# Query norms applied to the scores, the window mask added by TensorE, and a shifted TensorE loop in an AdaLN block

## The chip, the cores and the metric

The kernel runs on one core of a Trainium2 chip. The metric is the device time of one execution in microseconds, lower is better. A core has five engines that take their instructions from queues of their own: TensorE (PE), VectorE (DVE), ScalarE (ACT), GpSimd (POOL) and SyncE (SP), which here starts the DMAs. They meet only at semaphores: an instruction may wait until a counter has a value, and may raise one when it is done.

## The reference

The block has two halves. The first is a layer norm with modulation and a causal attention of 16 heads over an input of 8 batches x 512 tokens x 128 columns. The second, which this change touches, is a stack of six layers of local attention and a gated feed-forward:

```python
q = l2norm(q) * qs                      # per token and head, 64 columns
k = l2norm(k) * ksc
q = q * cos * scale + rotate_half(q) * sin * scale
k = k * cos * inv + rotate_half(k) * sin * inv
sim = jnp.einsum('bhwie,bhwje->bhwij', bq, bk2) * QK_SCALE
sim = jnp.where(mask, -jnp.finfo(sim.dtype).max, sim)   # window of 32, one window back
attn = jax.nn.softmax(sim, -1)
out = jnp.einsum('bhwij,bhwje->bhwie', attn, bv2)
...
for i in range(DEPTH):                  # DEPTH = 6
    x = attn_layer(shift_tokens(x), ...) + x
    x = ffn_layer(shift_tokens(x), ...) + x
```

`l2norm` divides a head's 64 numbers by their norm. One number per token and head does it, so for the query it may be applied to the scores of that token and head as well as to the query itself.

## The kernel before

Three parts run one after the other: `modulated_attention` (names `at_...`), `local_stack` (names `st_...`) and `last_residual` (`lr_...`). Only the second is changed. It works on units: a unit is one batch in one layer, 6 x 8 = 48 of them. Units 0 and 1 and the last ones are written out; units 2 to 46 are 45 passes of a hardware loop (L292). A unit has four tiles of 128 tokens, t = 0 to 3, so there are 192 tiles.

The order of the work is written by hand in `jobs_of` (L247). In each step t TensorE does, in this order: `q` of tile t, `tq` (transposing the rotated query of tile t-1), `k`, `tk`, `v`, `ot` (transposing the attention output of tile t-3), `pt` (transposing the probabilities of t-2), `sim` (the scores of t-1, 32 small matmuls per tile, L457), one job of the feed-forward (`m2` at t = 0, none at t = 1, `y` at t = 2, `m1` at t = 3), `z` (the output projection of t-3), `o` (probabilities times values of t-2), and at t = 1 the three blocks `h` of the feed-forward's first matmul. Each job owns PSUM banks: `q` 0 and 1, `k` and `o` 4 and 5, `tq`, `v` and `sim` 2 and 3, `tk` and `pt` 6 and 7, `ot` 0 and 1, `m1`, `m2` and `y` 7, `z` 6. `slot_free` makes a job wait until what stood in its banks has been read.

Around it, in step t:
- ScalarE squares q (L537), copies the transposed query (L559), squares k, copies the transposed keys into a block-diagonal tensor (L568), takes the exponential of the scores of t-2 (L573), copies v (L582), `ot` (L592) and `pt` (L598), and computes the reciprocal norms' first guess (L545, L547).
- VectorE sums the squares (L668), multiplies q and k by the cosines (L672) and sines (L686), clamps the sums (L679), adds the mask to the scores of t-1 while it takes them out of PSUM (L707), takes their maximum (L711), and divides the attention output by the softmax's sum (L749 to L759). At t = 1 it begins with a product of the feed-forward's norm (L656) and later finishes that norm (L736); the products of `hid` are L769.
- GpSimd adds the two parts of the rotation (L789, for q and k), refines the reciprocal norms (L796 to L802), multiplies the rotated q and then k by them (L809, `normalise`), and subtracts the maximum from the scores of t-1 (L837). At t = 1 it first does four operations for the feed-forward's norm (L816 to L824).

TensorE's `tq` waits for `normed[0]`, raised by the product for q in L809; `tk` for `normed[1]`.

Of the kernel before, what the change touches and what calls it, by code (L numbers as in the profile page):

```python
# [7 lines left out]
ALU = mybir.AluOpType  # L8
# [33 lines left out]

MASKED = -3.0e38


# [8 lines left out]


def shape_constants():

# [7 lines left out]
    first = seen & ((np.arange(P)[:, None] >= WIN) | (j >= WIN))  # L65
    c[:, C_MASK:C_MASK + 2 * WIN] = np.where(first, 0.0, MASKED)
    c[:, C_MASK + 2 * WIN:C_MASK + 4 * WIN] = np.where(seen, 0.0, MASKED)
    c[:, C_CAUSAL:C_CAUSAL + P] = np.where(np.arange(P)[None, :] <= np.arange(P)[:, None], 0.0, MASKED)
# [43 lines left out]
def local_stack(nc, w, LAYERS, const_sb, xT, x_done, w_split, tables):  # L112
# [68 lines left out]
    with ExitStack() as ctx:  # L181
# [36 lines left out]
        hid = sb("hid", [P, HC, N])  # L218

        ps = ctx.enter_context(nc.psum_tensor("st_ps", [P, NBANKS * BANK], F32))  # L220


        small_in, wo_in, w12_in = sem("small_in"), sem("wo_in"), sem("w12_in")
        wqkv_in = {k: sem(f"w{k}_in") for k in "qkv"}
# [16 lines left out]
        ff_squared, ff_rstd, ff_xn = sem("ff_squared"), sem("ff_rstd"), sem("ff_xn")  # L241
        gelu_ready = sem("gelu_ready")
        ff_gain, ff_newton, pool_own = sem("ff_gain"), sem("ff_newton"), sem("pool_own")
# [43 lines left out]

        def loop(eng, unit):

            unit(0)  # L290
            unit(1)
            with eng.Fori(2, NU - 1) as u:  # L292
                unit(u)
            unit(NU - 1)
            unit(NU)
            unit(NU + 1)

        with nc.Block() as block:
# [101 lines left out]
            def _(pe):  # L400
                pe.wait_ge(zeroed, 2)

                pe.sem_inc(ready["o"], 2)

                def unit(u):
                    for t in range(TILES):
                        at = STARTS[t]

                        for i, ((kind, d, index), _) in enumerate(jobs_of(t)):
# [29 lines left out]
                            elif kind in ("tq", "tk"):  # L439

                                pe.wait_ge(normed[kind == "tk"], tiles_done(u, d, index))
                                src = qk_rot[:, (kind == "tk") * INNER:(1 + (kind == "tk")) * INNER]
# [7 lines left out]
                            elif kind == "sim":  # L450
# [3 lines left out]
                                for c in range(IC):  # L454
                                    for g in range(WPT):
                                        key = index * P + g * WIN
                                        last = pe.matmul(  # L457
                                            out[g * WIN:(g + 1) * WIN, c * P:(c + 1) * P],
                                            qT[:, par, c * P + g * WIN:c * P + (g + 1) * WIN],
                                            k_bd[:, c, :, key:key + 2 * WIN], start=True, stop=True)  # L460
                            elif kind == "o":
# [43 lines left out]

                loop(pe, unit)

            @block.scalar
            def _(act):

                act.preload_act_table_set(EXP_LN_SET)
                act.wait_ge(small_in, 64)
                act.wait_ge(zeroed, 3)

                def round_half(u, d, half):
# [12 lines left out]
                def unit(u):  # L528
                    for t in range(TILES):
# [9 lines left out]
                        def reciprocal_norm():  # L539

                            act.wait_ge(ss_ready, n)
                            if not (start and n < 3):
                                act.wait_ge(normed[1], n - 2)
                            r = rn[:, t % 2, :]
                            act.activation(r, ss[:, t % 2, :], ACT.Ln, scale=SS_SCALE).then_inc(rn_ready, 1)  # L545
# [80 lines left out]

                loop(act, unit)

            @block.vector
            def _(dve):  # L630
# [17 lines left out]
                def unit(u):  # L648
                    start = isinstance(u, int)
                    for t in range(TILES):  # L650
# [7 lines left out]
                        def rotate(a):  # L658
# [7 lines left out]
                            if not (start and n < 3):  # L666
                                dve.wait_ge(normed[a], n - 2)
                            dve.tensor_reduce(nt[:, 2 + par, heads], qk_sq[:, cols].rearrange("p (h d) -> p h d", d=DH),  # L668
# [30 lines left out]
                        if alive(u, d1):  # L699
# [72 lines left out]

                loop(dve, unit)

            @block.gpsimd
            def _(pool):
                pool.wait_ge(small_in, 64)

                def unit(u):
                    start = isinstance(u, int)  # L780
                    for t in range(TILES):
# [57 lines left out]

                loop(pool, unit)  # L840

# [19 lines left out]
def modulated_attention(nc, w, const_sb, mod, xT, x_done, x1_dram, w_split, tables):  # L861
# [28 lines left out]
    with ExitStack() as ctx:  # L890
# [40 lines left out]
        ps_m = bank("m")  # L931

        w_in, x_in, x1_out, scale_in = sem("w_in"), sem("x_in"), sem("x1_out"), sem("scale_in")
        tables_done, tables_out = sem("tables_done"), sem("tables_out")
# [32 lines left out]

        def loop(eng, batch):

            batch(-1)  # L970
            batch(0)
            with eng.Fori(1, BATCH - 1) as b:
                batch(b)
            batch(BATCH - 1)
            batch(BATCH)

        with nc.Block() as block:
# [59 lines left out]
            def _(pe):  # L1037
# [103 lines left out]

                loop(pe, batch)

            @block.scalar
            def _(act):
# [71 lines left out]

                loop(act, batch)

            @block.vector  # L1220
            def _(dve):
# [162 lines left out]

                loop(dve, batch)

            @block.gpsimd
            def _(pool):
# [40 lines left out]

                loop(pool, batch)  # L1430

# [113 lines left out]
```

## Time and profile before

| what | value |
| --- | --- |
| runs of the kernel | 4410.03, 4414.46, 4418.47 us, median 4414.46 |
| the profiled execution | 4412.12 us, its span 4410.3 us |
| TensorE clock granted, mean | 0.959 of full speed |
| PE busy | 3768.9 us (85%) |
| PE's weight loads busy | 2856.2 us (65%) |
| DVE busy | 3571.7 us (81%) |
| ACT busy | 2656.4 us (60%) |
| POOL busy | 2895.4 us (66%) |
| `sim` matmuls, L457 | 376.1 us |
| q, k, v matmuls, L429 | 956.7 us |
| POOL's products with the norms, L809 | 722.7 us, x384 |

The span runs from the first to the last instruction of the profiled execution. The stack begins at about 880 us; its loop runs from about 1019 to 4250 us. A busy share is an average over the whole program; what a change is worth must be read where the engines wait for each other.

### The profile page before, as it was taken

What the parts mean: (1) busy time and instruction counts of PE and PEld (TensorE: products, weight loads), DVE (VectorE), ACT (ScalarE), POOL (GpSimd) and SP (SyncE); (2) the same over time, 40 slices, a digit from 0 to 9 for tenths busy, and PEclk for the clock granted to TensorE, in tenths of its full rate; (3) what the DMA queues carried; (4) which work ended last, traced back from release to release, by engine and by line L of the source; (5) the groups of instructions that cost most, each with busy time, mean ns of one, the idle gap of its engine ahead of it and who ended that gap; (6) DMA issues with size and microseconds to landing.
All of it is one profiled execution on the core that took longest, in us unless ns stands there. A gap on an engine that the chain in (4) does not pass through costs nothing. (4 is left out here: it accounts for less than half of the span.)

```text
span 4410.3 us, 109941 instructions
## 1 busy us (share of the span) xinstructions
PE 3768.9 (85%) x41516; PEld 2856.2 (65%) x41516; DVE 3571.7 (81%) x5298; ACT 2656.4 (60%) x4035; POOL 2895.4 (66%) x2520
## 2 busy tenths in 40 slices
PE   5666666669999899998999989999899999899996
PEld 3444444357777777776777767777677777677774
DVE  6777777678888788887888878888888888888884
ACT  5666666546666566656566656656566656566663
POOL 3555555357777677676767666777677676667672
PEclk9888888889999999999999999999999999999998
DMA  1111111032222322223222232222322222222221
GB/s 38 53 53 53 53 53 45 8 90 64 55 60 56 92 59 62 56 58 91 62 55 62 56 88 65 55 58 54 89 60 67 56 56 78 70 60 63 56 55 58
DMA packets 157205, 267.21 MB, mean 61 GB/s; under 512 B 32062, under 2 KB 51644, under 8 KB 152380
## 3 DMA queue, kind: packets, MB, share of 16 engines
q1 hardware_dynamic: 157116, 266.19, 22.1%
q8 instruction: 36, 0.59, 0.1%
q14 instruction: 53, 0.43, 0.0%
HBM read 44.81 MB, written 26.21 MB: 16 GB/s over the span
## 5 line engine op out<-in xcount | busy, mean ns | idle before, releaser
L789 POOL TENSOR_TENSOR st_qk_rot<-st_qk_rot,st_qk_sq 128x1024 f32<-128x1024 f32 x384 | 920.4, 2397 | 939.6 <-DVE st_qk_sq L686 939.6
L429 PE MATMUL st_ps<-st_wqkv,st_xs 128*128 128x512 f32 x3456 | 956.7, 412 | 66.2 <-DMA st_wqkv<-wqkv_parts 37.7
L537 ACT ACTIVATE st_qk_sq<-st_ps 128x1024 f32<-128x1024 f32 x384 | 393.9, 1026 | 652.6 <-PE st_ps L429 652.0
L429 PEld LDWEIGHTS st_ps<-st_wqkv,st_xs 128*128 128x128 f32 x3456 | 612.4, 190 | 231.4 <-issue 97.8
L809 POOL TENSOR_TENSOR st_qk_rot<-st_qk_rot,st_rn 128x1024 f32<-128x1024 f32 x384 | 722.7, 1903 | 15.0
L1426 POOL TENSOR_TENSOR at_probs<-at_probs,at_rden 128x128 f32<-128x128 f32 (+3 forms) x512 | 361.8, 738 | 389.6 <-DVE at_rden L1357 389.6
L668 DVE TENSOR_REDUCE st_nt<-st_qk_sq 128x16 f32<-128x1024 f32 x384 | 465.7, 1213 | 175.5 <-ACT st_qk_sq L537 175.4
L686 DVE TENSOR_TENSOR st_qk_sq<-st_ps,st_rot 128x512 f32<-128x512 f32 x768 | 490.2, 678 | 0.0
L672 DVE TENSOR_TENSOR st_qk_rot<-st_ps,st_rot 128x1024 f32<-128x1024 f32 x384 | 465.9, 1213 | 8.6 <-PE st_ps L444 8.6
L444 PE MATMUL st_ps<-consts_sb,st_qk_rot 128*128 128x128 f32 x3072 | 403.0, 274 | 27.9 <-DVE st_hid L769 16.5
L437 PEld LDWEIGHTS st_ps<-st_oT,st_wo 128*128 128x128 f32 x3072 | 368.8, 192 | 79.4 <-issue 75.8
L1191 ACT ACTIVATE at_probs<-at_score,at_nmx 128x128 f32<-128x128 f32 (+3 forms) x512 | 269.1, 527 | 249.0 <-DVE at_nmx L1347 244.3
L444 PEld LDWEIGHTS st_ps<-consts_sb,st_qk_rot 128*128 128x128 f32 x3072 | 357.1, 141 | 93.7 <-DVE st_hid L769 36.3
L568 ACT ACTIVATE st_k_bd<-st_ps 64x1024 f32<-64x1024 f32 x384 | 389.4, 1014 | 3.7 <-PE st_ps L444 1.4
L437 PE MATMUL st_ps<-st_oT,st_wo 128*128 128x128 f32 x3072 | 379.2, 277 | 1.4 <-ACT st_probT L598 1.2
L457 PE MATMUL st_ps<-st_k_bd,st_qT 128*32 128x128 f32 x12288 | 376.1, 275 | 1.8 <-ACT st_v_tok L582 1.8
L1056 PE MATMUL at_score<-at_k,at_qm 128*128 128x128 f32 (+3 forms) x512 | 239.9, 510 | 159.8 <-ACT at_probs L1191 117.6
L469 PE MATMUL st_ps<-st_v_bd,st_probT 128*32 128x128 f32 x12288 | 375.2, 274 | 0.0
L837 POOL TENSOR_TENSOR st_s<-st_s,st_mx 128x1024 f32<-128x1024 f32 x192 | 365.8, 1905 | 9.9 <-DVE st_mx L711 9.9
L707 DVE TENSOR_TENSOR st_s<-st_ps,consts_sb 128x1024 f32<-128x1024 f32 x192 | 234.5, 1221 | 146.4 <-PE st_ps L457 146.4
L457 PEld LDWEIGHTS st_ps<-st_k_bd,st_qT 128*32 128x32 f32 x12288 | 324.4, 110 | 34.4 <-ACT st_v_tok L582 26.2
L469 PEld LDWEIGHTS st_ps<-st_v_bd,st_probT 128*32 128x32 f32 x12288 | 323.8, 110 | 23.0
(125 smaller groups left out, 6828.4 us busy)
## 6 DMA issues: line engine op xcount, KB each, us to landing
st_v_bd<-st_v_tok SPq DMA_DIRECT2D x1152, 128.0 KB, 2.3
st_v_bd<-st_v_tok SPq DMA_DIRECT2D x672, 64.0 KB, 2.1
wqkv_parts<-at_w_parts SPq DMA_DIRECT2D x18, 1024.0 KB, 4.5
st_wqkv<-wqkv_parts SPq DMA_DIRECT2D x18, 1024.0 KB, 5.7
at_w_raw<-in_wqkv SPq DMA_DIRECT2D x18, 512.0 KB, 4.1
rotary_tables<-at_rot SPq DMA_DIRECT2D x6, 512.0 KB, 2.8
st_rot<-rotary_tables SPq DMA_DIRECT2D x24, 128.0 KB, 2.4
st_wo<-in_wo SPq DMA_DIRECT2D x6, 512.0 KB, 4.2
```

Source lines behind the costliest of these rows:

```text
L429: last = pe.matmul(out[:, c * 512:(c + 1) * 512], xs[:, x_part, t * P:(t + 1) * P], rhs, start=(n == 0), stop=(n == len(PASSES) - 1))
L437: last = pe.matmul(out[:, 0:P], wo[:, c, :], oT[:, c * P:(c + 1) * P], start=(c == 0), stop=(c == IC - 1))
L444: last = pe.transpose(out[:, c * P:(c + 1) * P], src[:, c * P:(c + 1) * P], ident)
L457: last = pe.matmul(out[g * WIN:(g + 1) * WIN, c * P:(c + 1) * P], qT[:, par, c * P + g * WIN:c * P + (g + 1) * WIN], k_bd[:, c, :, key:key ...
L469: last = pe.matmul(out[g * WIN:(g + 1) * WIN, c * P:(c + 1) * P], probT[:, c * P + g * WIN:c * P + (g + 1) * WIN], v_bd[:, par, g, :, c * ...
L537: act.activation(qk_sq[:, cols_of(a)], slot_of("qk"[a], 0, t), ACT.Square).then_inc(squared[a], 1)
L568: last = act.activation(k_bd[rows, :, a, WIN + t1 * P:WIN + (t1 + 1) * P], src[rows, :, :], ACT.Copy)
L668: dve.tensor_reduce(nt[:, 2 + par, heads], qk_sq[:, cols].rearrange("p (h d) -> p h d", d=DH), AX.X, ALU.add).then_inc(ss_sum, 1)
L672: dve.tensor_tensor(qk_rot[:, cols].rearrange("p (h d) -> p h d", d=DH), slot_of("qk"[a], 0, t).rearrange("p (h d) -> p h d", d=DH), rot[: ...
L686: last = dve.tensor_tensor(dst[:, :, g, :], src[:, :, 1 - g, :], sines.unsqueeze(1).to_broadcast([P, HEADS, DH // 2]), ALU.mult)
L789: pool.tensor_tensor(qk_rot[:, cols], qk_rot[:, cols], qk_sq[:, cols], ALU.add).then_inc(rot_done[a], 1)
L809: pool.tensor_tensor(view, view, rn[:, par, heads_of(a)].unsqueeze(2).to_broadcast([P, HEADS, DH]), ALU.mult).then_inc(normed[a], 1)
```

## The change

Four things are changed in `local_stack`:

1. GpSimd no longer multiplies q by its reciprocal norms; `tq` waits for the rotation of q alone (`rot_done[0]`).
2. VectorE's instruction that takes the scores out of PSUM multiplies them by those norms, broadcast over 64 columns, instead of adding the mask. Three waits go with it, since the norms are now read later.
3. The mask is added by TensorE: behind the 32 small matmuls of `sim`, which now leave their accumulation open, two matmuls multiply the identity (128 x 128) with the mask, broadcast over eight heads (512 columns), into the same banks. The mask's value becomes -1e30. ScalarE writes the identity and the two masks once as float32r, and TensorE waits for this.
4. 139 instructions that raise a semaphore nobody waits for stand on TensorE's queue before unit 0 (`ST_FILL`).

```diff
+AT_FILL = {}
+ST_FILL = {"pe": 139}
+def fill_block(eng, filled, n):
+    for _ in range(n):
+        eng.sem_inc(filled, 1)
...
+        ident_r, mask_r = sb("ident_r", [P, P], F32R), sb("mask_r", [P, 2, 2 * WIN], F32R)
...
-        def loop(eng, unit):
-
+        def loop(eng, unit, fill=0):
+
+            fill_block(eng, filled, fill)
             unit(0)
...
                 pe.wait_ge(zeroed, 2)
+                pe.wait_ge(rounded, 3)
...
-                                pe.wait_ge(normed[kind == "tk"], tiles_done(u, d, index))
+                                pe.wait_ge(normed[1] if kind == "tk" else rot_done[0], tiles_done(u, d, index))
...
-                                            k_bd[:, c, :, key:key + 2 * WIN], start=True, stop=True)
+                                            k_bd[:, c, :, key:key + 2 * WIN], start=(c % 4 == 0), stop=False)
+                                for c in range(2):
+                                    last = pe.matmul(out[:, c * 512:(c + 1) * 512].rearrange("p (h k) -> p h k", k=2 * WIN),
+                                                     ident_r[:, :],
+                                                     mask_r[:, index > 0, :].unsqueeze(1).to_broadcast([P, HEADS // 2, 2 * WIN]),
+                                                     start=False, stop=True)
...
+                act.activation(ident_r[:, :], ident, ACT.Copy).then_inc(rounded, 1)
+                for i in range(2):
+                    act.activation(mask_r[:, i, :], mask[i], ACT.Copy).then_inc(rounded, 1)
...
                                 act.wait_ge(normed[1], n - 2)
+                                act.wait_ge(taken["sim"], n - 2)
...
-                                dve.wait_ge(normed[a], n - 2)
+                                dve.wait_ge(rn_final, n - 2)
...
+                            dve.wait_ge(rn_final, n - 1)
                             dve.tensor_tensor(scores, slot_of("sim", d1, t1).rearrange("p (h k) -> p h k", h=HEADS),
-                                              mask[0 if t1 == 0 else 1].unsqueeze(1).to_broadcast([P, HEADS, 2 * WIN]),
-                                              ALU.add).then_inc(taken["sim"], 1)
+                                              rn[:, par, heads_of(0)].unsqueeze(2).to_broadcast([P, HEADS, 2 * WIN]),
+                                              ALU.mult).then_inc(taken["sim"], 1)
...
                             reciprocal_norms()
-                            normalise(0)
                             normalise(1)
```

How TensorE's queue moves, in the loop's pass at t = 2 (`st_s` are the scores, `st_o` the attention output, `st_hid` the feed-forward's hidden values). Before:

```order
L477 MATMUL st_ps<-consts_sb,st_o 128x128 x8
L449 MATMUL st_ps<-consts_sb,st_s 128x128 x8
L457 MATMUL st_ps<-st_k_bd,st_qT 32x128 x32
L502 MATMUL st_ps<-st_hid,st_w 128x512 x3
L437 MATMUL st_ps<-st_oT,st_wo 128x128 x8
```

and in the changed kernel, whose line numbers are higher:

```order
L499 MATMUL st_ps<-consts_sb,st_o 128x128 x8
L466 MATMUL st_ps<-consts_sb,st_s 128x128 x8
L474 MATMUL st_ps<-st_k_bd,st_qT 32x128 x32
L479 MATMUL st_ps<-st_mask_r,st_ident_r 128x512 x2
L524 MATMUL st_ps<-st_hid,st_w 128x512 x3
L454 MATMUL st_ps<-st_oT,st_wo 128x128 x8
```

The two matmuls with the mask stand between the scores and the next job, in all four steps; nothing else has moved there.

GpSimd's queue in one step, before (`st_qk_rot` is the rotated q and k, `st_rn` the norms, `st_mx` the maxima):

```order
L789 TENSOR_TENSOR st_qk_rot<-st_qk_rot,st_qk_sq 128x1024 x2
L793 REGISTER_ALU
L796 TENSOR_TENSOR st_nt<-st_rn 128x32
L797 ISA
L798 TENSOR_TENSOR st_nt<-st_nt,st_ss 128x32
L799 REGISTER_ALU
L800 TENSOR_TENSOR st_nt<-consts_sb,st_nt 128x32
L802 TENSOR_TENSOR st_rn<-st_rn,st_nt 128x32
L809 TENSOR_TENSOR st_qk_rot<-st_qk_rot,st_rn 128x1024 x2
L837 TENSOR_TENSOR st_s<-st_s,st_mx 128x1024
```

and in the changed kernel:

```order
L816 TENSOR_TENSOR st_qk_rot<-st_qk_rot,st_qk_sq 128x1024 x2
L820 REGISTER_ALU
L823 TENSOR_TENSOR st_nt<-st_rn 128x32
L824 ISA
L825 TENSOR_TENSOR st_nt<-st_nt,st_ss 128x32
L826 REGISTER_ALU
L827 TENSOR_TENSOR st_nt<-consts_sb,st_nt 128x32
L829 TENSOR_TENSOR st_rn<-st_rn,st_nt 128x32
L836 TENSOR_TENSOR st_qk_rot<-st_qk_rot,st_rn 128x1024
L863 TENSOR_TENSOR st_s<-st_s,st_mx 128x1024
```

One product of 128 x 1024 less stands ahead of the subtraction of the maxima.

## Rows read from the trace of the kernel before

**Rows 1.** Busy time by stretch: the stack's loop, 1110 to 4250 us.
```profile
1110.00:4250.00 3140.00, 2884.59 (x34868) 2260.20 (x34871) 2657.69 (x3280) 1929.19 (x2361) 2215.11 (x1750) 0.99 0.25 64
```
**Rows 2.** Waits, whole run: engine, line, waited for, total us, times, longest.
```profile
PE st_ps L477 <- issue: 112.3, 183, 1.6
...
PE st_ps L449 <- ACT st_s L573: 86.8, 145, 2.4
...
PEld st_ps L502 <- ACT st_probT L598: 18.6, 46, 0.4
...
PEld st_ps L486 <- ACT st_probT L598: 16.8, 41, 0.4
```
**Rows 3.** Timeline of TensorE, one pass: start us, us, instruction, idle before.
```profile
3076.22 1.96 PE L457 MATMUL st_ps<-st_k_bd,st_qT 128*32 128x128 f32 x64
3078.32 2.84 PE L502 MATMUL st_ps<-st_hid,st_w 128*128 128x512 f32 x6
...
3087.05 1.63 PE L429 MATMUL st_ps<-st_wqkv,st_xs 128*128 128x512 f32 x6
3088.52 1.03 PE L444 MATMUL st_ps<-consts_sb,st_qk_rot 128*128 128x128 f32 x8
...
3093.90 1.95 PE L457 MATMUL st_ps<-st_k_bd,st_qT 128*32 128x128 f32 x64
3095.84 1.12 PE L481 MATMUL st_ps<-xT_sb,consts_sb 128*128 x2
3096.80 1.95 PE L437 MATMUL st_ps<-st_oT,st_wo 128*128 128x128 f32 x16
...
3124.33 1.07 PE L477 MATMUL st_ps<-consts_sb,st_o 128*128 128x128 f32 x8 [1.61 <-issue]
3125.24 1.04 PE L449 MATMUL st_ps<-consts_sb,st_s 128*128 128x128 f32 x8
3126.20 1.95 PE L457 MATMUL st_ps<-st_k_bd,st_qT 128*32 128x128 f32 x64
3128.09 2.05 PE L437 MATMUL st_ps<-st_oT,st_wo 128*128 128x128 f32 x16
...
3132.26 1.12 PE L494 MATMUL st_ps<-st_xc,st_w 128*128 128x512 f32 x2 [0.24 <-DVE st_xc L736]
```
**Rows 4.** Timeline of VectorE in the same pass, from the end of t = 0.
```profile
3117.18 1.23 DVE L759 TENSOR_TENSOR st_o<-st_ps,st_den 128x1024 f32<-128x1024 f32 x1
3118.32 2.46 DVE L656 SCALAR_TENSOR_TENSOR st_xc<-st_xc,st_ln_g,st_rstd 128x512 f32<-128x512 f32 x1
...
3122.96 1.27 DVE L686 TENSOR_TENSOR st_qk_sq<-st_ps,st_rot 128x512 f32<-128x512 f32 x2
...
3129.09 1.21 DVE L707 TENSOR_TENSOR st_s<-st_ps,consts_sb 128x1024 f32<-128x1024 f32 x1
```
**Rows 5.** Timeline of GpSimd over the same time.
```profile
3114.60 3.77 POOL L809 TENSOR_TENSOR st_qk_rot<-st_qk_rot,st_rn 128x1024 f32<-128x1024 f32 x2
3118.32 1.91 POOL L837 TENSOR_TENSOR st_s<-st_s,st_mx 128x1024 f32<-128x1024 f32 x1
3120.19 1.49 POOL L816 TENSOR_TENSOR st_xc<-st_rstd 128x512 f32<-128x512 f32 x1
```
**Rows 6.** Timeline of ScalarE at t = 1 of the same pass.
```profile
3123.47 1.06 ACT L573 ACTIVATE st_s<-st_s 128x1024 f32<-128x1024 f32 x1
```
**Rows 7.** One line's instructions, L656: duration ns min/median/max, first and last start.
```profile
L656 DVE SCALAR_TENSOR_TENSOR st_xc<-st_xc,st_ln_g,st_rstd x48: 741/2473/2498, 1037.6 to 4363.6; 128x512 f32<-128x512 f32 x48
```
**Rows 8.** Who waited for GpSimd's products L809, whole run: us, times.
```profile
  PE st_ps L444: 11.3, 3
```
**Rows 9.** One line's instructions, L403: TensorE's queue raises a semaphore.
```profile
L403 PEldq EVENT_SEMAPHORE  x1: 51/51/51, 895.8 to 895.8; - x1
```
**Rows 10.** DMA queues over the whole run: packets, MB, share.
```profile
q8 instruction: 36, 0.59, 0.1%
```
**Rows 11.** The same for 1110 to 4260 us: the only instruction queue listed.
```profile
q14 instruction: 3, 0.02, 0.0%
```

More of the change, by code:

```diff
@@ L43 @@
 MASKED = -3.0e38
+MASKED_SCORE = -1.0e30
 C_IDENT, C_MEAN, C_MASK, C_CAUSAL = 0, P, 2 * P, 2 * P + 4 * WIN
@@ L65, in shape_constants @@
     first = seen & ((np.arange(P)[:, None] >= WIN) | (j >= WIN))
-    c[:, C_MASK:C_MASK + 2 * WIN] = np.where(first, 0.0, MASKED)
-    c[:, C_MASK + 2 * WIN:C_MASK + 4 * WIN] = np.where(seen, 0.0, MASKED)
+    c[:, C_MASK:C_MASK + 2 * WIN] = np.where(first, 0.0, MASKED_SCORE)
+    c[:, C_MASK + 2 * WIN:C_MASK + 4 * WIN] = np.where(seen, 0.0, MASKED_SCORE)
     c[:, C_CAUSAL:C_CAUSAL + P] = np.where(np.arange(P)[None, :] <= np.arange(P)[:, None], 0.0, MASKED)
@@ L218, in local_stack @@
         hid = sb("hid", [P, HC, N])
+        ident_r, mask_r = sb("ident_r", [P, P], F32R), sb("mask_r", [P, 2, 2 * WIN], F32R)
         ps = ctx.enter_context(nc.psum_tensor("st_ps", [P, NBANKS * BANK], F32))
+        filled = sem("filled")
         small_in, wo_in, w12_in = sem("small_in"), sem("wo_in"), sem("w12_in")
@@ L241, in local_stack @@
         ff_squared, ff_rstd, ff_xn = sem("ff_squared"), sem("ff_rstd"), sem("ff_xn")
-        gelu_ready = sem("gelu_ready")
+        gelu_ready, rounded = sem("gelu_ready"), sem("rounded")
         ff_gain, ff_newton, pool_own = sem("ff_gain"), sem("ff_newton"), sem("pool_own")
@@ L504, in unit @@
                             last.then_inc(ready[kind], 1)
-                loop(pe, unit)
+                loop(pe, unit, ST_FILL.get('pe', 0))
             @block.scalar
@@ L625, in unit @@
                             act.preload_act_table_set(EXP_LN_SET)
-                loop(act, unit)
+                loop(act, unit, ST_FILL.get('act', 0))
             @block.vector
@@ L771, in unit @@
                                                          ALU.add, ALU.mult).then_inc(taken["h"], 1)
-                loop(dve, unit)
+                loop(dve, unit, ST_FILL.get('dve', 0))
             @block.gpsimd
@@ L838, in unit @@
                                                ALU.subtract).then_inc(shifted, 1)
-                loop(pool, unit)
+                loop(pool, unit, ST_FILL.get('pool', 0))
 AH = 16
@@ L931, in modulated_attention @@
         ps_m = bank("m")
+        filled = sem("filled")
         w_in, x_in, x1_out, scale_in = sem("w_in"), sem("x_in"), sem("x1_out"), sem("scale_in")
@@ L966, in jobs_at, with loop @@
                     if (step, p) == (s % AH, part) and (not kinds or kind in kinds)]
-        def loop(eng, batch):
+        def loop(eng, batch, fill=0):
+            fill_block(eng, filled, fill)
             batch(-1)
@@ L1140, in batch @@
                         m_products(b, s, 1)
-                loop(pe, batch)
+                loop(pe, batch, AT_FILL.get('pe', 0))
             @block.scalar
@@ L1216, in batch @@
                                     take(b, job)
-                loop(act, batch)
+                loop(act, batch, AT_FILL.get('act', 0))
             @block.vector
@@ L1383, in batch @@
                             finish_norm(b, -1, True)
-                loop(dve, batch)
+                loop(dve, batch, AT_FILL.get('dve', 0))
             @block.gpsimd
@@ L1428, in batch @@
                         last.then_inc(weights_ready, 1)
-                loop(pool, batch)
+                loop(pool, batch, AT_FILL.get('pool', 0))
 def last_residual(nc, const_sb, mod, xT, x1_dram, out):
```

## The prediction

> **What bounds the kernel now.** First I read the busy time by stretch. In the 3140 us from 1110 to 4250 TensorE is busy 2885 us, 92%, at a granted clock of 0.99 (its level of 2.4 GHz); VectorE has 85%, GpSimd 71%, ScalarE 61% [rows 1]. So the loop is close to TensorE's own time, and the question is what ends TensorE's few gaps. The view of waits names two: before `ot` (L477) it stands 112.3 us in 183 cases, before `pt` (L449) 86.8 us in 145 cases, for the exponential [rows 2]. "issue" on the first hides a wait: `ot` takes the banks of q, so it needs VectorE's sine product of q (L686), and the timeline shows that one end at 3122.96 + 1.27 = 3124.23 and `ot` start at 3124.33 [rows 3, 4]. Neither chain (q matmul, square, sum, two products; k matmul, square, key copy, exponential) has GpSimd in it. GpSimd's products with the norms, of which the change removes half, made anyone wait for 11.3 us in 3 cases in the whole run [rows 8]. What GpSimd gives up is thus off the path, but for one place that the timeline shows at t = 1, below.
>
> **The mask pair on TensorE.** Two float32r matmuls of 512 columns per tile. The nearest row is the projection: six of that shape and type from 3087.05 to the next start at 3088.52, 1.47/6 = 0.245 us each [rows 3]; the pair costs m = 0.49 us. Below it could only go if they overlapped the scores; above, a float32 matmul of 512 columns took 3096.80 - 3095.84 = 0.96 us [rows 3], so a pair of 1.92 us if the broadcast mask streamed at that pace. I take 0.49, with 0.45 to 0.60 as its own range: same engine, type and width. 192 tiles would make 94 us, but each of the four steps of a pass must be walked, S being how much later TensorE is than before, from `h` of one pass to `h` of the next.
>
> - t = 2: behind the scores comes `y`, which waits for ScalarE's copy L598 [rows 2]: from the scores' start to its start 2.10 us (3076.22, 3078.32), against 1.88 where nothing is waited for (3126.20, 3128.09) [rows 3]. The pair fills that 0.22: +0.27.
> - t = 3: scores to `m1` 1.94 us (3093.90, 3095.84), 0.06 hidden: +0.43. S = 0.70.
> - t = 0: `m2` waits for the same copy as `y` (16.8 us in 41 cases, beside 18.6 in 46 [rows 2]): +0.27. S = 0.97.
> - t = 1: `ot` stood 1.61 us [rows 3], since VectorE was late: L759 ended and L656 took 2.46 us instead of the 0.74 that is its minimum [rows 4, 7]. It ended 0.6 us after GpSimd's L837 did (3118.32 + 1.91 = 3120.23; 3120.78) [rows 4, 5]: it had to let that instruction, which reads SBUF too, go first.
>
>  With the change VectorE reaches L656 at 3118.32 + S(t = 3) 0.70 + m 0.49 = 3119.51. GpSimd, also 0.70 later but one product (3.77/2 = 1.88 us) shorter [rows 5], ends L837 at 3120.23 + 0.70 - 1.88 = 3119.05 and goes on with L816, 1.04 to 1.49 us. L656 then waits for that instead: it ends at about 3119.1 + 1.2 + 0.6 = 3120.9, as late as before. So `ot` keeps its time and the 0.97 is swallowed. Late next is the exponential: it ended at 3123.47 + 1.06 = 3124.53 [rows 6], is S later, 3125.50, and 0.1 us behind it (as `ot` behind L686) `pt` can start, 3125.60 against 3125.24: +0.36. The pair follows: +0.85 at `z`. `h` waited about 0.31 us for VectorE's L736 (from `z` to `h` 3132.26 - 3128.09 = 4.17 us, where `z` and `o` fill 1.98 + 1.88) [rows 3]; that wait goes: +0.54, with the roundings 0.56.
>
> In a formula the next `h` is 4m - 1.4 us later, 0.56 with m = 0.49. 46 passes of full content make 25.8 us. Two units of the ramps without a feed-forward pay nearly the full 4m: +3.5.
>
> The Trainium skill (SBUF — State Buffer, section "SBUF: two separate sides") states that VectorE and GpSimd share one pair of ports as an exclusive lock, held for the whole instruction, so that a VectorE operation with two SBUF inputs fully blocks behind a GpSimd one. The trace agrees for L656: 2.46 us against 0.74. By that rule L679, a small clamp, also shortens at t = 1, which is not late for anyone and changes no term.
>
> **VectorE's product instead of the sum.** Same shape, PSUM in, one SBUF operand broadcast. The product with the softmax's reciprocal (L759), of just that form, took 1.23 us, the sum 1.21 us [rows 4]: nothing, +-0.02 x 192 = 4 us at most, and VectorE waits for the scores in three steps of four. At t = 1, where L707 stood right behind L686 (3129.09), it now finds the scores ready at about 3129.0: no loss. The wait for the norms is behind GpSimd's work of the step before; behind it queue the maximum and `z`'s addition, but it is met long before the scores are. ScalarE's new wait for `taken["sim"]` asks for a tile two back. Both cost nothing.
>
> **Start of the stack.** 139 semaphore instructions; the nearest row is 51 ns for one that TensorE's queue executed [rows 9]: 7.1 us, at most; at least 0, if they pass while TensorE waits for its first input. They stand behind the wait for ScalarE's rounding, so little is left to hide them: I take +6.5. Against it stand the 11.3 us [rows 8] that `tq` and `tk` waited for the products in the first tiles: the change takes 1.9 us off each `tk` and more off `tq`; I take -6. Bounds for both together: -11 to +8. Sum: 25.8 + 3.5 + 0.5 = +30 us.
>
> **Where the loop stands.** Queue q8 moved 36 packets in the whole run, 16 KB each, and none from 1110 to 4260 us [rows 10, 11]. I read it as TensorE's program: its loop is held on the chip, and moving it to a border can gain nothing against before. It can only keep that state, since a pass grows by 16 instructions. The Trainium skill (Runtime: NRT & Kernel Launch, "Instruction fetch mechanics") says that a taken branch whose target is outside a window of two blocks of 256 instructions forces a fetch; TensorE's pass, some 1,670 instructions, would then be fetched anew 45 times. The empty q8 in rows 11 speaks against it for TensorE.
>
> The profiled execution took 4412.12 us (span 4410.3 and 1.8 around it); the median of the runs is 2.3 us above it, less than their spread. 4412.1 + 30 = 4442 us.
>
> **Rivals.**
> - A, the forecast: m from 0.45 to 0.60 gives 0.40 to 1.00 us a pass, 18 to 46 us, with the rest (+4) 4434 to 4462.
> - B, faster: the pair costs TensorE less than it replaces in gaps. It decides from 4m = 1.4, m = 0.35. For it: 64 narrow score matmuls leave room between them, and wide ones might slip in. Against: they come behind the scores in one queue, and 512 columns took 0.245 us each with no gap between them. At m = 0.20: -0.60 x 46 = -28, with the rest 4388.
> - N, no change: m near 0.35, or the start gives back all of the 11.3 us; 4404 to 4421.
> - D, t = 1 swallows nothing: L656 starts 1.19 us later and still takes 2.46 us, because GpSimd goes on with its next instruction before it gives way. Then `ot` is 1.19 later, and a pass 1.19 + 0.49 - 0.31 = 1.37 us: 63 us, with the rest 4479. For it: GpSimd's operations stand nearly without gaps. Against: L656 did get in between L837 and L816.
> - C, the change doesn't do what it says: the loop now touches one block too many, and TensorE fetches in each pass. The trace of before shows no such stall; 36 packets took 0.1% of 16 engines' span [rows 10], 0.05 to 0.15% before rounding, so 1 to 3 us each; one waited for per pass is 45 us or more on top of A: 4487 and up.
> - E, the mask streams at the float32 pace: 4 x 1.92 - 1.4 = 6.3 us a pass, 4706.
>
> **Chances.** A 0.50, D 0.15, C 0.07, E 0.03, N 0.11, B 0.14. A measurement of this kernel tells 0.2%, 9 us, from nothing. A, D, C and E are slower by more: 0.75; N 0.11; B 0.14. The range takes in A, D and N and part of B and C: 4398 to 4492, with A's own 4434 to 4462.
>
> **What would show it.** The new matmuls at 0.24 to 0.25 us from start to start; the pair's 0.49 between the scores and `y`, `m1`, `m2`, `z`; `y` and `m2` no longer waiting for L598; L656 at 1.2 to 1.6 us; `ot` at t = 1 with a gap of 0.6 us in place of 1.6, and a new gap of 0.2 us for the exponential before `pt`; L736 no longer named before `h`; a pass 0.6 us longer; no q8 packet in the loop. I am wrong if a pass is shorter than before, which would need a gap before `ot` or `pt` in t = 2, 3 or 0 to have shrunk, or if TensorE's queue stalls at the loop's branch.

## The result and the profile after

The changed kernel takes 4520.64 us (median of 4 runs, 4516.04 to 4530.03), the kernel before in the same session 4413.16 us: ratio 1.0245, 95% interval [1.0225, 1.0265]. It is 107 us slower. The prediction was 4442 us, range 4398 to 4492: the sign was right, the size 3.6 times too small.

The same stretch of the loop as in [rows 1], then the page's engine line. Columns of the first: TensorE, its weight loads, VectorE, ScalarE and GpSimd busy, the granted clock, the DMA share, GB/s.

```profile
1110.00:4250.00 3140.00, 2887.94 (x34403) 2267.68 (x34402) 2559.82 (x3193) 1874.07 (x2300) 1840.87 (x1539) 0.99 0.24 63
```
```profile
PE 3867.7 (86%) x41900; PEld 2930.7 (65%) x41900; DVE 3537.3 (78%) x5298; ACT 2652.3 (59%) x4038; POOL 2532.3 (56%) x2328
```

TensorE is as full as before, at the same clock, with 1.3% fewer instructions in the stretch; GpSimd has given up 374 us of work there, and yet a pass is longer, as the next rows show.

One pass of TensorE, from `h` to `h`. This is the counterpart of [rows 3]; columns: start, duration, instruction, and in brackets the gap before it and what ended it.

```profile
3070.02 5.41 PE L516 MATMUL st_ps<-st_xc,st_w 128*128 128x512 f32 x12 [1.17 <-DVE st_xc L763]
...
3102.83 1.95 PE L474 MATMUL st_ps<-st_k_bd,st_qT 128*32 128x128 f32 x64
3104.72 0.73 PE L479 MATMUL st_ps<-st_mask_r,st_ident_r 128*128 128x512 f32 x2
3105.29 1.02 PE L503 MATMUL st_ps<-xT_sb,consts_sb 128*128 x2
3106.15 1.95 PE L454 MATMUL st_ps<-st_oT,st_wo 128*128 128x128 f32 x16
...
3132.85 1.06 PE L499 MATMUL st_ps<-consts_sb,st_o 128*128 128x128 f32 x8 [0.51 <-issue]
3134.31 1.07 PE L466 MATMUL st_ps<-consts_sb,st_s 128*128 128x128 f32 x8 [0.39 <-ACT st_s L599]
3135.30 1.95 PE L474 MATMUL st_ps<-st_k_bd,st_qT 128*32 128x128 f32 x64
3137.19 0.73 PE L479 MATMUL st_ps<-st_mask_r,st_ident_r 128*128 128x512 f32 x2
3137.76 1.95 PE L454 MATMUL st_ps<-st_oT,st_wo 128*128 128x128 f32 x16
3139.63 1.96 PE L491 MATMUL st_ps<-st_v_bd,st_probT 128*32 128x128 f32 x64
3142.77 5.41 PE L516 MATMUL st_ps<-st_xc,st_w 128*128 128x512 f32 x12 [1.18 <-DVE st_xc L763]
```

A pass takes 3142.77 - 3070.02 = 72.75 us. Before, the `h` at 3132.26 [rows 3] followed this one, 70.93 us earlier:

```profile
3061.33 5.41 PE L494 MATMUL st_ps<-st_xc,st_w 128*128 128x512 f32 x12 [0.24 <-issue]
```

All but every eighth pass of either kernel repeat these lengths, with medians of 72.74 and 70.95 us; the eighth, where the layer changes, is 7 to 8 us longer before and 8 to 9 us longer after. So a pass pays 1.79 us, 45 x 1.79 = 81 us, where I had forecast 0.56. The five layer changes pay about 1 us each on top of it.

The gap before `ot` at t = 1 has shrunk to 0.51 us and a gap of 0.39 us stands before `pt`, as forecast. What is new is the last row: `h` waits 1.18 us for VectorE's L763 (L736 in the kernel before). The waits of the whole run, to be read beside [rows 2]; columns: who waits, for whom, us in total, times, longest:

```profile
PE st_ps L466 <- ACT st_s L599: 100.5, 186, 2.1
...
PE st_ps L499 <- issue: 68.0, 181, 0.6
...
PE st_ps L516 <- DVE st_xc L763: 53.4, 45, 1.2
...
PE st_ps L446 <- issue: 46.8, 1, 46.8
```

45 passes, 53.4 us. Why L763 is late stands in VectorE's and GpSimd's timelines of this pass. VectorE:

```profile
3128.23 1.06 DVE L682 SCALAR_TENSOR_TENSOR st_xc<-st_xc,st_ln_g,st_rstd 128x512 f32<-128x512 f32 x1
...
3134.93 0.45 DVE L705 TENSOR_SCALAR st_ss<-st_nt 128x32 f32<-128x32 f32 x1
3135.30 1.27 DVE L712 TENSOR_TENSOR st_qk_sq<-st_ps,st_rot 128x512 f32<-128x512 f32 x2
3137.95 1.22 DVE L734 TENSOR_TENSOR st_s<-st_ps,st_rn 128x1024 f32<-128x1024 f32 x1 [1.38 <-PE st_ps L479]
3139.21 1.22 DVE L738 TENSOR_REDUCE st_mx<-st_s 128x16 f32<-128x1024 f32 x1
3140.35 2.11 DVE L763 TENSOR_SCALAR st_xc<-st_xc,st_ln_b 128x512 f32<-128x512 f32 x1
```

GpSimd:

```profile
3127.70 1.04 POOL L843 TENSOR_TENSOR st_xc<-st_rstd 128x512 f32<-128x512 f32 x1
...
3136.65 2.37 POOL L816 TENSOR_TENSOR st_qk_rot<-st_qk_rot,st_qk_sq 128x1024 f32<-128x1024 f32 x1 [1.31 <-DVE st_qk_sq L712]
...
3140.28 1.90 POOL L836 TENSOR_TENSOR st_qk_rot<-st_qk_rot,st_rn 128x1024 f32<-128x1024 f32 x1
```

GpSimd's product of k with the norms (L836) began at 3140.28, VectorE's L763 0.07 us later. L763 ended at 3142.46, 0.28 us after L836 had (3142.18). In the kernel before, L736 took 0.48 us, at 3131.47, and GpSimd's products began only at 3133.10, 1.15 us after it had ended. These are its rows at t = 1, three of VectorE's and one of GpSimd's; the first is the clamp, L705 in the changed kernel:

```profile
3126.41 1.57 DVE L679 TENSOR_SCALAR st_ss<-st_nt 128x32 f32<-128x32 f32 x1
3127.90 1.27 DVE L686 TENSOR_TENSOR st_qk_sq<-st_ps,st_rot 128x512 f32<-128x512 f32 x2
...
3131.47 0.48 DVE L736 TENSOR_SCALAR st_xc<-st_xc,st_ln_b 128x512 f32<-128x512 f32 x1
```
```profile
3133.10 3.76 POOL L809 TENSOR_TENSOR st_qk_rot<-st_qk_rot,st_rn 128x1024 f32<-128x1024 f32 x2
```

Over the whole run (duration ns min/median/max), after and before:

```profile
L763 DVE TENSOR_SCALAR st_xc<-st_xc,st_ln_b x48: 486/2110/2140, 1076.4 to 4482.0; 128x512 f32<-128x512 f32 x48
```
```profile
L736 DVE TENSOR_SCALAR st_xc<-st_xc,st_ln_b x48: 476/477/517, 1050.8 to 4368.8; 128x512 f32<-128x512 f32 x48
```

Their first and last starts also split the loss. From the first to the last is 3405.6 us against 3318.0: 88 us in the passes and ramps. The first comes 25.6 us later. Of this, 8.9 us lie ahead of the stack, in a part that the change doesn't touch (ScalarE's first instruction of the stack stands at 886.90, before at 878.03); the profiles here differ there by up to 19 us, in no order that goes with an edit. Another 21.1 us lie between that instruction and TensorE's first matmul, and 4.4 us are won from there on. At that matmul stand the fillers, to be read beside [rows 9], and TensorE's first matmul behind them:

```profile
L65 PEldq EVENT_SEMAPHORE  x139: 51/51/51, 905.6 to 926.8; - x139
```
```profile
927.02 3.32 PE L446 MATMUL st_ps<-st_wqkv,st_xs 128*128 128x512 f32 x7 [46.78 <-issue]
```

Each takes 51 ns, as forecast, but from the first to the last start 21.2 us pass over 138 steps: 0.154 us each. The same matmul began at 897.01 before.

Queue q8 brings TensorE's instructions, as the variant without filler will show. It moved one packet between 1110 and 4250 us, 37 in the run (36 before [rows 10]), so TensorE still runs its loop without fetching. The same window after the change:

```profile
q8 instruction: 1, 0.02, 0.0%
```

### The profile page after: what moved, and what is told of

Read it like the earlier page. It is cut to its first block and busy times, and to the rows that moved or that the text cites. A ratio compares the mean times of both kernels' runs of the same rounds, so it can differ in the third digit from the quotient of the medians.

```text
span 4521.1 us, 110514 instructions
## 1 busy us (share of the span) xinstructions
PE 3867.7 (86%) x41900; PEld 2930.7 (65%) x41900; DVE 3537.3 (78%) x5298; ACT 2652.3 (59%) x4038; POOL 2532.3 (56%) x2328
## 5 line engine op out<-in xcount | busy, mean ns | idle before, releaser
L816 POOL TENSOR_TENSOR st_qk_rot<-st_qk_rot,st_qk_sq 128x1024 f32<-128x1024 f32 x384 | 921.4, 2400 | 1403.1 <-DVE st_qk_sq L712 1403.1
L734 DVE TENSOR_TENSOR st_s<-st_ps,st_rn 128x1024 f32<-128x1024 f32 x192 | 235.2, 1225 | 305.5 <-PE st_ps L479 305.5
L836 POOL TENSOR_TENSOR st_qk_rot<-st_qk_rot,st_rn 128x1024 f32<-128x1024 f32 x192 | 365.3, 1902 | 15.0
```

The costliest lines, as they stand in the source:

```text
L816: pool.tensor_tensor(qk_rot[:, cols], qk_rot[:, cols], qk_sq[:, cols], ALU.add).then_inc(rot_done[a], 1)
```

## Experiments

Each run is compared with the kernel before, run alongside on the same chip (4411 to 4414 us). A pass is the median distance between successive `h` (x12 matmuls) in that run's timeline. The first five runs vary the changed kernel. Two questions stood open: is it the collision of L763 with GpSimd's product that costs the extra 1.2 us, and does the filler cost 21 us for nothing?

**Take the collision away, first way.** VectorE finishes the norm before the sine product of k, instead of behind the maximum of the scores:

```diff
+                            if a == 1 and t == 1 and alive(u, -2):
+                                finish_ff_norm(u)      # the wait and L763's tensor_scalar
                             dve.tensor_tensor(...)     # k's sine product
...
-                            dve.wait_ge(ff_newton, units_done(u, -2, 4, 3))
-                            dve.tensor_scalar(xc[:, :], xc[:, :], 0.5, column(ln_b, P, layer_of(u, -2)), ALU.mult,
-                                              ALU.add).then_inc(ff_xn, 1)
```

> The changed kernel with VectorE's end of the feed-forward norm (L763, xc * 0.5 + ln_b) moved at t = 1 from behind the maximum to between the clamp and the sine product of k. Theory L (port): in its old place it was taken up at 3140.35 while GpSimd's product with k's norms ran 3140.28 to 3142.14, took 2.11 us in place of 0.48, and the blocks h waited 1.18 us for it; in the new place GpSimd is between two operations, so it takes 0.5 us, the gap before h is gone, a pass is 71.55 us and the time 4521 - 53 = 4468 us. Rival M (size of the pair alone): the time is the two new matmuls at more than 0.49 us, and L763 is slow in itself; it takes 2.1 us in the new place too and a pass stays within 0.3 us of 72.7, 4521 us.

Measured: 4460.12 us, ratio 1.0108 [1.0091, 1.0125]: 60.5 us less than the changed kernel. A pass is 71.49 us, 1.25 less. The moved instruction is back at 0.47 us:

```profile
L676 DVE TENSOR_SCALAR st_xc<-st_xc,st_ln_b x48: 473/474/485, 1064.0 to 4415.1; 128x512 f32<-128x512 f32 x48
```

and `h` no longer has a gap (two successive ones of TensorE's timeline):

```profile
3095.89 5.42 PE L516 MATMUL st_ps<-st_xc,st_w 128*128 128x512 f32 x12
...
3167.37 5.42 PE L516 MATMUL st_ps<-st_xc,st_w 128*128 128x512 f32 x12
```

**Second way: take GpSimd's instruction away.** L763 stays where it is; GpSimd leaves out the product of k with its norms in the tiles of t = 1, and only signals.

```diff
-                            normalise(1)
+                            if t == 1:
+                                pool.wait_ge(rn_final, n)
+                                pool.wait_ge(rot_done[1], n)
+                                pool.sem_inc(normed[1], 1)
+                            else:
+                                normalise(1)
```

> The changed kernel, with GpSimd's product of k with its norms left out in the tiles t = 1 (their k stays unscaled); VectorE's L763 stays where it was. Theory L (port): with no GpSimd operation running when L763 is taken up, it takes 0.48 us as in the kernel before, the gap of 1.18 us before h goes, a pass is 71.55 us and the time 4468 us. Rival M: L763 and the pass stay as they are, 4521 us; GpSimd's work has no part in it.

Measured: 4461.48 us, ratio 1.0106 [1.0089, 1.0123], a pass of 71.48 us. L763 is untouched in its place, and short:

```profile
L763 DVE TENSOR_SCALAR st_xc<-st_xc,st_ln_b x48: 476/477/486, 1074.7 to 4421.0; 128x512 f32<-128x512 f32 x48
```

The two edits have nothing in common but that the two instructions no longer coincide, and they give the same time. This shows the cause.

**Third way: another engine.** ScalarE does L763's work.

```diff
+                            act.wait_ge(ff_newton, units_done(u, -2, 4, 3))
+                            act.activation(xc[:, :], xc[:, :], ACT.Identity, scale=0.5,
+                                           bias=column(ln_b, P, layer_of(u, -2))).then_inc(ff_xn, 1)
```

> The changed kernel with the end of the feed-forward's norm (xc * 0.5 + ln_b) on ScalarE, behind its reciprocal norms at t = 1, where it stood idle for over 5 us. Theory L: ScalarE's reads do not meet GpSimd's; the gap before h goes as in the version that moved it on VectorE, a pass is 71.55 us, 4460 us. Rival: h then waits for something else that was hidden behind L763 (the h banks, VectorE's o product), and a pass is over 72 us.

Measured: 4464.82 us, ratio 1.0109 [1.0093, 1.0125], a pass of 71.50 us. The same again.

**The filler, moved.** The 139 updates stand ahead of TensorE's wait for the zeroed tiles, where it idles anyway.

```diff
+                fill_block(pe, filled, ST_FILL.get('pe', 0))
                 pe.wait_ge(zeroed, 2)
...
-                loop(pe, unit, ST_FILL.get('pe', 0))
+                loop(pe, unit)
```

> The changed kernel with the same 139 instructions ahead of TensorE's wait for the zeroed buffers, where TensorE stood idle for 25 us. Same number of instructions ahead of the loop, so the loop lies as in the changed kernel. Theory F: 139 x 0.154 = 21.4 us pass from about 887 us on, ending near 908, so the first projection starts about 18 us earlier: 4503 us, a pass unchanged at 72.7 us. Rival: the spacing of 0.154 us comes from something else that runs at that moment, and the sum of the start stays as it was, 4521 us.

Measured: 4499.57 us, ratio 1.0199 [1.0182, 1.0216]: 21 us less, 3 more than forecast. Nearly the whole of the filler's time had been exposed. In this trace the updates run from 876.4 to 897.5 us and the first q matmul starts at 897.93. From the start of the last matmuls of the part before the stack to that q matmul are 30.0 us, against 48.3 in the changed kernel and 27.5 in the kernel before; so 2.5 us are still exposed.

**The filler, taken away.** `ST_FILL = {}`.

> The changed kernel without the 139 filler instructions. Theory F (filler is only a delay at the start): in the changed kernel they ran from 905.6 to 926.8 us, 0.154 us from one to the next, while the first input was ready at about 906.3; without them the first projection starts some 20 us earlier and the time is 4521 - 20 = 4500 us, with a pass of the stack's loop still 72.7 us and no instruction packet of queue q8 in it. Rival B (the loop needs the border): without the filler a pass ends so close to a block's end that TensorE fetches instructions in every pass; packets of q8 then stand in the loop, a pass is at least 1 us longer, and the time is 4521 - 20 + 45 x 1 = 4546 us or more.

Measured: 4720.72 us, ratio 1.0705 [1.0687, 1.0723]. Here theory F was wrong by 220 us, and rival B holds, with a price far above its lower bound. A pass is 78.46 us. q8 from 1110 to 4400 us, and TensorE's queue at the first q of a pass (timeline, then the whole run):

```profile
q8 instruction: 375, 6.14, 0.9%
```
```profile
3063.37 2.44 PE L446 MATMUL st_ps<-st_wqkv,st_xs 128*128 128x512 f32 x6 [4.09 <-issue]
```
```profile
PE st_ps L446 <- issue: 188.6, 44, 4.7
```

Some nine packets come in each pass, and TensorE stands still for 4.3 us at the first q. The stall costs clock too: the granted clock is 1.00 ahead of it (3055 to 3059 us) and 0.57 behind it (3063.4 to 3067.1 us), and the six q matmuls take 2.44 us there. Since L763 took 477 ns in the median of this run, the collision is no part of its pass: the fetch costs 78.46 - 71.49 = 6.97 us a pass, not the 5.7 between the two kernels. The longer loop does need the filler, or another way to its place.

**Is it the length or the place?** The kernel before, with 139 and with 30 updates ahead of its loop.

```diff
-                loop(pe, unit)
+                loop(pe, unit, 139)                    # the second run: 30
```

> The kernel before with nothing changed but 139 semaphore updates on TensorE ahead of its loop, placed as in the changed kernel (behind the wait for the zeroed tiles). In the built program its loop then stands at TensorE instructions 5328 to 6984 instead of 5189 to 6845. If a loop of this length runs without fetching wherever it stands, only the 139 updates count: about 20 us more than before, 4433 us, a pass of 70.95 us and almost no packets on q8 between 1110 and 4250 us. If it is the number of blocks of 256 instructions touched that decides (with the start-up instructions that the run puts ahead, this position touches one more block than before's, as the variant without filler did), the pass stalls for a fetch as there: 4.3 to 4.7 us of waiting at the start of q's or another job in each pass, 8 to 9 packets of q8 a pass, about 5.7 us more a pass, 4413 + 20 + 45 x 5.7 = about 4690 us. Between them: 4560 us.

Measured: 4430.96 us, ratio 1.0041 [1.0026, 1.0057], a pass of 70.95 us, one packet of q8 from 1110 to 4250 us. My block rule, as I had it, was wrong by 260 us; the 139 updates cost 20 us. But the rule had an assumed number in it, the instructions that stand ahead of the program at run time. With 48 to 66 of them in place of 20, one rule fits all four places seen: a loop that touches 7 blocks stays, one that touches 8 is fetched. That gave a place for the next run where the rule and the length disagree.

> The kernel before with 30 semaphore updates on TensorE ahead of its loop instead of none: the loop of 1657 instructions stands at 5219 to 6875 of the built program. It ran without fetches at 5189 (before) and at 5328 (139 updates), and the changed kernel's loop of 1673 ran without them at 5356 and with them at 5217. One rule fits all four: the loop runs free if it touches 7 blocks of 256, and fetches if it touches 8, provided that the run puts 48 to 66 instructions ahead of what the built program shows (I had assumed about 20, and so got the last expectation wrong). By this rule 5219 touches 8 blocks: 8 to 9 packets of q8 a pass, about 5.7 us more a pass, 4412 + 5 + 45 x 5.7 = about 4675 us. The rival (the length decides: 1657 instructions fit wherever they stand, 1673 only at a border; or executing some semaphore updates has nothing to do with it): 4412 + 30 x 0.154 = 4417 us, a pass of 70.95 us and no packets of q8 in the passes.

Measured: 4651.06 us, ratio 1.0536 [1.0517, 1.0555], a pass of 77.07 us. From 1110 to 4400 us, and one of its passes:

```profile
q8 instruction: 338, 5.54, 0.8%
```
```profile
3118.29 2.92 PE L433 MATMUL st_ps<-st_wqkv,st_xs 128*128 128x512 f32 x6 [4.13 <-issue]
```

The same 1657 instructions run free at 5189 and 5328 of the built program and are fetched in each pass at 5219: 30 instructions that wait for nothing cost 238 us. It is the place. Behind the stall the granted clock is 0.50, its level of 1.2 GHz, from 3118.3 to 3121.0 us, where it was 1.00 ahead of it (3110 to 3114 us). That the border count is 7 blocks of 256 against 8 is an inference that fits five places, one of them forecast; the 48 to 66 instructions ahead were fitted, not seen.

**The mask pair alone.** The changed kernel without the two mask matmuls (the scores are not masked) and without filler; and the kernel before with the pair and the filler, q still scaled by GpSimd (VectorE still adds the mask, so it is added twice). The first run's edit, where the matmuls of the scores also close their accumulation again:

```diff
-                                for c in range(2):
-                                    last = pe.matmul(out[:, c * 512:(c + 1) * 512]..., ident_r[:, :], mask_r[...],
-                                                     start=False, stop=True)
```

> The changed kernel without the two mask matmuls per tile (the scores are left unmasked) and without the filler; TensorE's program then lies as in the kernel before. What is left is the norm of q on the scores and GpSimd's relief. Theory L (port): the exponential bounds pt at t = 1 and the blocks h come after it: a pass is 70.95 - 0.9 = 70.05 us if L763 finds the port free, 4373 us; if it is still taken up just behind the start of GpSimd's L836, it costs 1.2 us again and the pass is about 71.2, 4425 us. Rival M (the pair's size alone makes the change slow, GpSimd's relief costs nothing): the pass is at or below 70.95 us and L763 takes 0.48 us, 4413 us or less.

Measured: 4371.87 us, ratio 0.9913 [0.9898, 0.9928], a pass of 70.10 us, with no gap before `h`.

> The kernel before, with the mask pair on TensorE and the 139 filler instructions alone: GpSimd scales q as before, VectorE still adds the mask too (twice the mask is the same mask). Theory L: the pair costs 0.47 us behind each tile's scores, of which the copy wait hides 0.22 twice and t = 1 a little; GpSimd is busy with its second product later, so L736 is not blocked; a pass is 70.95 + 0.86 = 71.8 us, with 21 us of filler at the start 4413 + 40 + 21 = 4474 us. Rival M: the pair alone makes the pass of the changed kernel, 72.7 us, and the time is 4520 us.

Measured: 4480.42 us, ratio 1.0152 [1.0137, 1.0168], a pass of 71.80 us.

So eight mask matmuls a pass cost 71.49 - 70.10 = 1.39 us where nothing collides. Relieving GpSimd of q is worth 0.85 without them; with them, 71.80 - 71.49 = 0.31 if L763 is out of the way, and a loss of 0.94 if it isn't.

These traces also show what it takes for the two instructions to meet. At t = 1 of one pass each, in us behind the start of the scores:

| kernel | clamp took | norm's last step starts | it took | GpSimd's next big product starts |
| --- | --- | --- | --- | --- |
| before | 1.57 | 5.27 | 0.48 | 6.90 |
| pair alone | 1.57 | 5.28 | 0.48 | 6.91 |
| changed, without the pair | 0.44 | 4.42 | 0.48 | 5.40 |
| changed | 0.45 | 5.05 | 2.11 | 4.98 |

Neither half of the change makes the collision. Taking q off GpSimd draws its product forward by 1.5 us, and still VectorE is done 0.5 us before it. The pair then holds VectorE's reading of the scores back by 0.6 us, into the product.

**Towards a faster kernel.** The kernel before, with the norm's last step on ScalarE, then also with the product L656 split between ScalarE (times the gain) and GpSimd (times the reciprocal deviation), so that VectorE has neither.

```diff
+                            act.activation(xc[:, :], xc[:, :], ACT.Copy,
+                                           scale=column(ln_g, P, layer_of(u, -2))).then_inc(ff_gain, 1)
...
+                            pool.tensor_tensor(xc2[:, :], xc2[:, :], rstd[:, :], ALU.mult).then_inc(ff_newton, 1)
```

> The kernel before with only the last step of the normalisation (L736, x times 0.5 plus bias) moved from VectorE to ScalarE. My theory (L736 is the last thing that h waits for at t = 1, 0.31 us a pass in the kernel before, and it shares a port with GpSimd): the gap of 0.31 us before h goes, 46 x 0.31 = 14 us, 4399 us, ratio 0.9968. The rival (the variant with both moves gained by the split of L656 alone, because ScalarE as the later engine delays h as much): 4413 us, ratio 1.000, with a gap before h that ends on ScalarE.

Measured: 4406.81 us, ratio 0.9987 [0.9978, 0.9996]. A pass is 70.64 us, 0.31 less, and `h` has no gap, as expected; from the first to the last `h` the profile has 11.7 us less than before, but of the 14 us forecast only 4 show in the medians. In its profile the first q matmul stood 6.5 us later (903.48, before 897.01), and ahead of it lies only a part that is the same in both; whether that part takes the gain in the other runs too is not shown.

> A version meant to beat both: the kernel before with both VectorE operations that meet GpSimd's port taken off VectorE. L656 (xc * ln_g * rstd) becomes a ScalarE copy scaled by ln_g at t = 0 and one more GpSimd product by rstd; L736 becomes a ScalarE activation at t = 1. Theory L: L656 took 2.46 us in place of 0.74 and bounded ot at t = 1; without it ot starts 1.4 us earlier, pt is bound by the exponential 0.6 us earlier, and the 0.31 us before h go: a pass is 70.95 - 0.9 = 70.05 us and the time 4413 - 41 = 4372 us. Rival (GpSimd becomes late): GpSimd's extra 1.28 us at t = 1 delays its rotations and the next tq; the pass stays at 70.95 us or grows.

Measured: 4382.70 us, ratio 0.9937 [0.9923, 0.995], a pass of 70.11 us. The pass is as forecast and the time 11 us above the 4372. It beats both kernels.

**The changed kernel mended**: the filler early, L763 on ScalarE, L682 split.

> The changed kernel with three edits: the 139 updates ahead of the wait for the zeroed tiles, the last normalisation step on ScalarE, and the normalisation's product L682 split between ScalarE and GpSimd. The two effects that I missed are 21 and about 60 us: 4520 - 21 - 60 = about 4440 us, with a pass of 71.5 us; the split adds nothing, since no matmul of the changed kernel waits for that product any more. If the effects overlap (the rival: the early updates delay the start of other queues, or the split relieves a wait), the sum misses by over 10 us. In any case it stays above the kernel before, by what the eight mask matmuls of a pass cost (ratio 1.006).

Measured: 4442.27 us, ratio 1.0068 [1.0052, 1.0083], a pass of 71.50 us. The two effects that I had missed add up. What is left is 71.50 - 70.95 = 0.55 us a pass: the pair's 1.39, less the 0.85 that relieving GpSimd gives back.

## Why the prediction was wrong

The sum of the loss by the runs: 107.5 us, of which 60.5 go with the collision and 21.1 with the place of the filler. The remaining 26 us (31 by the medians of the mended kernel, within the interval of its ratio) stand against the 25.8 + 3.5 that I had for the pair. The collision alone carries the time out of the range: without it 4460 us was measured, with the filler still in its place; without the filler's delay, but with the collision, 4500 us. By step:

- **The pair's price, m = 0.49: right.** It takes 0.57 us from its start to the next job's (3104.72, 3105.29), but the job behind it is 0.10 shorter: `m1` to `z` 0.86 us, 0.96 in [rows 3]. Net 0.47.
- **The waits it hides: right.** From scores to pair is 1.88 to 1.89 us in all four steps (2.10 to `y` at t = 2 [rows 3]); the waits for ScalarE's copy are gone at `y` and `m2`.
- **t = 1 swallows 0.97 us: right.** L682 took 1.06 us in place of 2.46 [rows 4]. `ot` waits 0.51 us (forecast 0.6) and `pt` 0.39 us for the exponential (forecast 0.2). L682 ended 0.55 us after GpSimd's L843 (3129.29, 3128.74), the instruction that I had it wait for. Rival D, a wait as long as before, fell. Without the collision a pass is 71.49 - 70.95 = 0.54 us longer; forecast 0.54 to 0.56.
- **"`h` waited about 0.31 us for VectorE's L736 ...; that wait goes": this step failed.** It grew to 1.18 us. Where it came from stands two paragraphs further on in the prediction: I had seen that the clamp L679 "also shortens at t = 1, which is not late for anyone and changes no term". By the traces it was the term, together with the pair (the table above). The clamp fell from 1.57 us to 0.45, and VectorE ended k's sine product 1.7 us earlier against the scores: 1.27 us behind their start (3136.57, 3135.30), not 2.97 (3129.17, 3126.20). The clamp gave 1.12 of this; the other 0.58 came because the scores now start 2.55 us behind the end of q's sine product in place of 1.97, held by the exponential. VectorE itself gained nothing further, since it then stood 1.38 us before L734 for TensorE's scores and pair. But GpSimd takes k's rotation from that product and ran as far ahead: its big product began 4.98 us behind the scores' start instead of 6.90, and L763 began 5.05 behind it (before: 5.27). It fell right behind the start of L836. With 1.12 us more in the clamp the product would have begun 6.10 us behind the scores' start, after L763 at 0.48 us had ended (5.53); that is an estimate from these rows, and no run has the clamp alone. I walked both engines up to the wait that I was interested in and stopped there.
- **The rule was in my hands.** The Trainium skill (SBUF — State Buffer, section "SBUF: two separate sides") has the lock between VectorE and GpSimd held for a whole instruction. I applied it to L656, where it gives time back, and not to L736, where it takes it. The Trainium skill has it there for VectorE operations with two SBUF inputs or in a two-port mode; L736 has one such input, and no trace names its mode. The traces agree with the lock at both places: 2.46 us to 1.06, and 0.48 to 2.11, the latter ending 0.28 us behind GpSimd's product.
- **"51 ns for one ...: 7.1 us, at most": this bound failed.** A record's duration is not the distance to the next. The filler's true spacing, 0.154 us, stood nowhere in the trace of before; 51 ns was the lower end of the term and I called it the upper. The sum lacked about 15 us for it. The 6 us that I credited to the first `tq` and `tk` came: their waits for GpSimd's products fell from 11.3 us [rows 8] to 3.9 for L836 and 0.9 for L816. From the first q matmul to the first L763 are 149.4 us (927.02, 1076.4), before 153.8 (897.01, 1050.8).
- **Where the loop stands: right against before, wrong in its reason.** No fetch in the loop, before or after. But I gave rival C, one block too many, little weight for the changed kernel, and then expected in the first experiments that the filler was idle. It is what keeps the loop free, and it is worth 200 us. The Trainium skill (Runtime: NRT & Kernel Launch, "Instruction fetch mechanics") gives TensorE's instruction memory as 2048 instructions, refilled in blocks of 256, and speaks of a window of two blocks for a taken branch. The first agrees with seven blocks that stay and eight that don't, if the next one is always fetched ahead; the two-block window doesn't hold for TensorE, whose loop of over six blocks ran for 3140 us, over 40 passes, on one packet or none.

## What to carry to other kernels

When a change makes an engine early, follow everything that it feeds to the end of the step: an engine that shares VectorE's port may arrive just in time to lock it, and the price can be nearly the whole of its instruction (1.6 of 1.9 us here), paid by whoever waits behind. Before trusting such a walk, list each VectorE operation on the path beside the GpSimd instruction that would run at its new time. A loop of TensorE that nearly fills its instruction memory should be timed at two or three places, since 30 instructions ahead of it cost 5% here; and filler belongs where the engine is waiting, at 0.154 us a piece.

## What the runs showed of the hardware

- A VectorE tensor_scalar of 128x512 (0.48 us) took 2.11 us when a GpSimd product (1.90 us) had started 0.07 us before it.
- 139 semaphore updates in a row on TensorE took 0.154 us each, though each record shows 51 ns.
- A loop of 1657 TensorE instructions ran with one instruction-queue packet or none in some 40 passes at two places, and with about eight packets and a stall of about 4 us per pass at a third, 30 instructions from the first. With 1673 instructions there was a free and a stalling place too. After the stall the granted clock was 0.50 to 0.57 for the next 3 to 4 us, 1.00 before it.
- Two float32r matmuls of 512 columns behind 32-column ones took 0.57 us until the next job started, 0.47 net.
